# An attention pipeline on one core: order within VectorE's step, units normalized in pairs, lags of 15 and 16 steps, three key or value units a step

## The reference, cut to what matters

```python
x = x + xattn(layernorm(x), ctx, ctx, Wq, Wk, Wv, Wo)   # x: 16 x 512 x 512, ctx: 16 x 120 x 512
x = x + ffn(layernorm(x), w_gate, w_up, w_down)         # inner width 1536, quantized steps
# xattn: 16 heads of 32; q and k are rotated (rope) before the scores
score = einsum('bhqd,bhkd->bhqk', qh, kh) / sqrt(32)
out   = einsum('bhqk,bhkd->bhqd', softmax(score), vh)   # then times Wo
# ffn: rounds x, up, gate, sigmoid(gate), gate*sig and gate*up to 16 bits, each with
# a scale from the largest magnitude of the whole tensor; weights to 4 bits in blocks of 32
```

## Time and profile before

| | us |
|---|---|
| median of three executions | 2526.41 |
| lowest, highest | 2521.74, 2530.59 |
| the profiled execution, its own time | 2532.82 |
| its span in the trace | 2530.9 |
| attention stage in it, up to the gate product's first matmul | 980.5 |

### The profile page before, as it was taken

One profiled execution on the slowest core, in us unless ns is written; L12 is line 12 of the kernel. 1 busy time (PEld: TensorE's weight loads), 2 busy tenths in 40 slices (PEclk: granted clock), 3 DMA queues, 4 the chain that ended last, 5 costly groups with the idle time before them and its releaser, 6 DMA issues.

```text
span 2530.9 us, 32312 instructions
## 1 busy us (share of the span) xinstructions
PE 2271.9 (90%) x12763; PEld 1005.0 (40%) x12763; DVE 1704.4 (67%) x1750; ACT 1285.3 (51%) x1184; POOL 627.8 (25%) x432
## 2 busy tenths in 40 slices
PE   5788887888788876999999989999999499999999
PEld 2443333333333322444444434444444244444444
DVE  5655776677677554664555348988888787777773
ACT  3334443444344311232232248778888597777771
POOL 3542443344334220110010015444444100000000
PEclk9988998999899988999999999999999799999999
DMA  7434445544544455779787569777787465555551
GB/s 206 114 91 119 131 124 145 150 133 128 148 148 125 147 149 161 224 230 290 246 258 245 183 202 369 291 284 283 289 289 290 185 234 216 216 216 218 223 222 69
DMA packets 307913, 505.57 MB, mean 200 GB/s; under 512 B 208172, under 2 KB 210476, under 8 KB 270892
## 3 DMA queue, kind: packets, MB, share of 16 engines
q1 hardware_dynamic: 307756, 503.45, 60.3%
HBM read 248.83 MB, written 186.65 MB: 172 GB/s over the span
## 4 chain that ended last, share of the span: by engine, by line
PE 66%; DVE 13%; DMA 7%; SPq 6%; issue 4%; ACT 2%; POOL 1%; DVEq 0%; POOLq 0%; ACTq 0%
PE banks L1220 39%; PE banks L1617 18%; DMA RB<-sr_s 4%; SPq L344 3%; DVE MX L967 2%; PE banks L562 2%; DVE XA L841 2%; SPq L354 2%; PE banks L520 2%; DVE RX L942 1%; DMA RG<-sr_s 1%; PE banks L483 1%; DVE st L825 1%; PE banks L480 1%; PE banks L539 1%
## 5 line engine op out<-in xcount | busy, mean ns | idle before, releaser
L1617 PE MATMUL banks<-W,OH 128*128 128x512 f16 x2304 | 500.9, 381 | 37.1 <-DVE OH L1696 37.1
L1220 PE MATMUL banks<-XB,W 128*128 128x512 f16 x2304 | 499.3, 380 | 22.7 <-DMA XB<-XC 22.7
L1220 PE MATMUL banks<-XB,WT 128*128 128x512 f16 x2304 | 499.9, 380 | 8.2 <-DMA XB<-xt_s 8.2
L1240 ACT ACTIVATE OB<-banks,uns 128x512 f32<-128x512 f32 x384 | 254.2, 683 | 427.7 <-PE banks L1220 421.1
L1617 PEld LDWEIGHTS banks<-W,OH 128*128 128x128 f16 x2304 | 226.0, 98 | 311.9 <-issue 39.1
L1220 PEld LDWEIGHTS banks<-XB,W 128*128 128x128 f16 x2304 | 225.8, 98 | 296.2 <-DMA XB<-XC 23.2
L1220 PEld LDWEIGHTS banks<-XB,WT 128*128 128x128 f16 x2304 | 225.9, 98 | 282.1 <-DMA XB<-xt_s 8.7
L562 PE MATMUL banks<-XC,AH 128*128 128x512 f16 x768 | 214.6, 439 | 106.5 <-DVE RX L942 106.5
L1485 POOL TENSOR_TENSOR PR<-GS,OB 128x2048 f32<-128x2048 f32 x47 | 226.2, 4814 | 273.0 <-ACT OB L1240 253.6
L1309 DVE TENSOR_REDUCE amx<-OB 128x1 f32<-128x2048 f32 x48 | 109.7, 2285 | 240.5 <-ACT OB L1240 240.5
L520 PE MATMUL banks<-XD,WQ 128*128 128x512 f16 x768 | 178.6, 383 | 0.0
(11 more groups left out here) (211 smaller groups left out, 2944.4 us busy)
## 6 DMA issues: line engine op xcount, KB each, us to landing
g_s<-OB SPq DMA_DIRECT2D x48, 1024.0 KB, 5.7
GL<-g_s SPq DMA_DIRECT2D x48, 1024.0 KB, 8.4
up_s<-OB SPq DMA_DIRECT2D x48, 1024.0 KB, 4.9
XA<-up_s SPq DMA_DIRECT2D x32, 1024.0 KB, 9.3
gq_s<-GQ SPq DMA_DIRECT2D x48, 512.0 KB, 5.1
XD<-gq_s SPq DMA_DIRECT2D x48, 512.0 KB, 6.7
XA<-in_x SPq DMA_DIRECT2D x16, 1024.0 KB, 7.6
QW<-QE SPq DMA_DIRECT2D x128, 128.0 KB, 2.8
```

Source lines behind the costliest of these rows:

```text
L1220: t = e.matmul(pk[:].rearrange("p (j t) -> p j t", j=4), WT[w][:, ot, wa, kk, :], XB[i % 2][:, xa, :, kk, :], start=(kk == 0 and wa == 0 a ...
L1240: e.activation(OB[n % 3][:, r, :], bank[k % 8][:], ACT.Copy, scale=uns[:, 12 * w + ot:12 * w + ot + 1]).then_inc(s_ev, 1)
L1617: t = e.matmul(pk[:].rearrange("p (r n) -> p r n", r=4), OH[i % 2][:, a, ot, j * 128:(j + 1) * 128], WD[:, :, c, wa, o4, :], start=(ot == ...
```

## The change

It rewrites the schedule of the attention stage and leaves the arithmetic as it is.

1. VectorE's step begins with X1, then the rotation's addition, then the normalization, then the statistics of X1. X1 and the output projection belong to units s-16 and s-15 (before: s-18 and s-17). The loop has 80 steps.
2. Units are normalized in pairs: two at c = 1 and two at c = 2 of a step, none at c = 3 and c = 0. Their broadcasts are issued one step earlier at the head of SP's step, eight DMAs together; the store of the reciprocals at c = 3 moves ahead of the transposing DMA and the load of x.
3. Key and value units: 8, then 3 in each of steps 0 to 6, 2 and 1 in steps 7 and 8. The largest magnitudes and splits that belong to them move with them (ctx3 to steps 1 and 2, Wo to 8 and 9, V to 9 and 10).
4. The first four rotations have four buffers (`qe`); the first swaps stand ahead of the first transposing DMA of x; the first loads wait for one another; GpSimd's two rotation products are split, with the low parts between them.
5. The transposing DMAs of the weights and loads of X1 for the next stage move two steps earlier, like `dve_normal` (68, 69 for 72, 74).

```diff
-NSTEP = NU + 18
-KV_STEPS = {-1: 8, 0: 3, 1: 3, 2: 2, 3: 2, 4: 2, 5: 2, 6: 2, 7: 2, 8: 2, 9: 2, 10: 2}
-AMAX = ("ctx0", "wk", "wv", "ctx1", "wq", "ctx2", "ctx3", "v", "wo")
+NSTEP = NU + 16
+KV_STEPS = {-1: 8, 0: 3, 1: 3, 2: 3, 3: 3, 4: 3, 5: 3, 6: 3, 7: 2, 8: 1}
+AMAX = ("ctx0", "wk", "wv", "ctx1", "wq", "ctx2", "ctx3", "wo", "v")
...
+def normal_at(s):
+
+    b, c = divmod(s - 13, 4)
+    return [4 * b + 2 * c, 4 * b + 2 * c + 1] if 0 <= b < B and c < 2 else []
...
+        def qe(n):
+            return (QE[0], QE[1], QR[6], QR[7])[n] if n < 4 else QE[n % 2]
...
         def kv_bank(i):
-            return 5 if i >= 24 or i % 2 == 0 else 6
+            return 5 if i >= 29 or i % 2 == 0 else 6
...
             sp_ctx_load(e, 0)
+            e.wait_ge(s_cx, 16)
             e.dma_start(WLD[0], wk.rearrange("(k p) e -> p k e", p=128)).then_inc(s_wld[0], 16)
             sp_x_load(e, 0)
+            e.wait_ge(s_wld[0], 16)
             e.dma_start(WLD[1], wv.rearrange("(k p) e -> p k e", p=128)).then_inc(s_wld[1], 16)
...
             sp_swap(e, 0, 4 * SK)
+            sp_swap(e, 1, 4 * SK)
             sp_x_turn(e, 0)
             sp_x_load(e, 1)
-            sp_swap(e, 1, 4 * SK)
...
-
-                u = s - 16
+                for u in normal_at(s + 1):
+                    sp_recip(e, u)
+
+                u = s - 14
...
-                u = s - 18
+                u = s - 16
                 if 0 <= u < NU:
                     e.wait_ge(s_x1, u + 1)
                     e.dma_start(x1_d[u // 4, :, u % 4, :], X1[u % 2]).then_inc(s_x1d[u % 2], 16)
...
-                if s == 1:
+                if s == 0:
                     sp_ctx_turn(e, 2)
                     sp_ctx_load(e, 3)
-                if s == 5:
+                if s == 3:
                     sp_ctx_turn(e, 3)
-                if s == 10:
+                if s == 7:
                     e.wait_ge(s_v, 12)
...
+                if c == 3 and 0 <= b - 2 < B:
+                    e.wait_ge(s_rr, 2 * (b - 1))
+                    e.dma_start(sr_d[1 + b % 2].rearrange("r (e f) -> (r e) f", f=64), RG[:]).then_inc(s_rd, 16)
 
                 if c == 1 and 1 <= b + 1 < B:
                     sp_x_turn(e, b + 1)
                 if c == 2 and 2 <= b + 2 < B:
                     sp_x_load(e, b + 2)
-                if 0 <= s - 12 < NU:
-                    sp_recip(e, s - 12)
...
-                if 0 <= s - 17 < NU:
-                    pe_output(e, s - 17)
+                if 0 <= s - 15 < NU:
+                    pe_output(e, s - 15)
...
-                u = s - 13
-                if 0 <= u < NU:
+                for u in normal_at(s):
                     nb, nc_ = divmod(u, 4)
                     e.wait_ge(s_an, u + 1)
...
             for s in range(NSTEP):
                 b, c = divmod(s, 4)
 
-                if s == 0:
-                    dve_x_shift(e, 1)
-                elif s <= NU:
-                    dve_rope_add(e, ROT["q", s - 1])
...
-                u = s - 18
+                u = s - 16
                 if 0 <= u < NU:
                     ob, j = divmod(u, 4)
                     e.wait_ge(s_o, u + 1)
...
                     e.scalar_tensor_tensor(X1[u % 2], BO_, vun[:, 2:3], XR[u % 2], ALU.mult, ALU.add).then_inc(s_x1, 1)
+
+                if s == 0:
+                    dve_x_shift(e, 1)
+                elif s <= NU:
+                    dve_rope_add(e, ROT["q", s - 1])
+                    for i in kv_at(s - 1):
+                        if i % 8 < 4:
+                            dve_rope_add(e, ROT["k", i])
+
+                for u in normal_at(s):
+                    e.wait_ge(s_rb[u % 2], 64 * (u // 2 + 1))
+                    e.wait_ge(s_a, u + 1)
+                    e.tensor_tensor(A[:, u % 6, :], A[:, u % 6, :], RB[u % 2][:], ALU.mult).then_inc(s_an, 1)
...
-                if s in (3, 5, 7):
-                    dve_v_max(e, (s - 3) // 2)
+                if s in (2, 4, 6):
+                    dve_v_max(e, (s - 2) // 2)
...
             for s in range(NSTEP):
                 b, c = divmod(s, 4)
-                u = s - 13
-                if 0 <= u < NU:
+                if s < NU:
+                    pool_rope_cosine(e, ROT["q", s])
+                for u in normal_at(s):
...
                 if s < NU:
-                    pool_rope(e, ROT["q", s])
+                    pool_rope_sine(e, ROT["q", s])
```

More of the change, by code:

```diff
@@ L468, in pe_kv @@
             pk = bank[kv_bank(i)]
-            before = i - 1 if i > 24 else i - 2
+            before = i - 1 if i >= 29 else i - 2
             if before >= 0:
@@ L609, in pe_attention @@
                     pe_queries(e, s)
-                if s == 0:
[L611 to L614, removed]
+                if amax is not None:
+                    if amax == 7:
+                        kv_empty(e, 31)
+                    pe_amax(e, amax)
                 for i in kv[:1]:
@@ L618, in pe_attention @@
                     pe_largest(e, s - 2)
-                if s in (5, 11, 12):
-                    pe_amax_all(e, {5: 6, 11: 7, 12: 8}[s])
+                if amax is not None:
+                    pe_amax_all(e, amax)
                 if c == 2 and 0 <= b - 1 < B:
@@ L645, in act_rope_in @@
         def act_rope_in(e, n):
-            if n >= 2:
-                e.wait_ge(s_rm1, n - 1)
-                e.wait_ge(s_qw[n % 2], 32 * (n // 2))
+            if n >= 4:
+                before = n - 4 if n < 6 else n - 2
+                e.wait_ge(s_rm1, before + 1)
+                e.wait_ge(s_qw[n % 2], 32 * (before // 2 + 1))
         def act_kv(e, i):
@@ L970, in dve_attention @@
                     dve_ctx_low(e, 2)
-                if s == 5:
+                if s == 1:
+                    dve_ctx_max(e, 3)
+                if s == 2:
                     dve_ctx_unit(e, 3)
@@ L1043, in pool_rope @@
                 to = KR[i // 8][:, i % 8, :].rearrange("p (b s) -> p b s", b=4)
-                cc, ss = (a[:].unsqueeze(1).to_broadcast([128, 4, SK]) for a in (ck, sk))
+                cc = ck[:].unsqueeze(1).to_broadcast([128, 4, SK])
             e.wait_ge(s_qe, n + 1)
@@ L1049, in pool_rope, with pool_rope_sine @@
                 e.wait_ge(s_c1, i - 7)
-            e.tensor_tensor(to, v(QE[n % 2]), cc, ALU.mult).then_inc(s_rm1, 1)
+            e.tensor_tensor(to, v(qe(n)), cc, ALU.mult).then_inc(s_rm1, 1)
+        def pool_rope_sine(e, n):
+            what, i = ROTS[n]
+            if what == "q":
+                v, ss = (lambda a: a[:]), sq[:]
+            else:
+                v, ss = (lambda a: a[:, 0:4 * SK].rearrange("p (b s) -> p b s", b=4)), sk[:].unsqueeze(1).to_broadcast([128, 4, SK])
             e.wait_ge(s_qw[n % 2], 32 * (n // 2 + 1))
@@ L1076, in pool_attention @@
             pool_deviation(e, 0)
[L1077 to L1079 removed]
+            pool_rope_cosine(e, 0)
+            pool_rope_sine(e, 0)
+            pool_rope_cosine(e, 1)
+            pool_rope_sine(e, 1)
+            pool_rope_cosine(e, 2)
+            pool_rope_sine(e, 2)
             pool_deviation(e, 1)
[L1081 removed]
+            pool_rope_cosine(e, 3)
+            pool_rope_sine(e, 3)
             for s in range(NSTEP):
                 b, c = divmod(s, 4)
[L1084 to L1085 removed]
+                if s < NU:
+                    pool_rope_cosine(e, ROT["q", s])
+                for u in normal_at(s):
                     nb, nc_ = divmod(u, 4)
@@ L1089, in pool_attention @@
                 if s < NU:
-                    pool_rope(e, ROT["q", s])
+                    pool_rope_sine(e, ROT["q", s])
                 for i in kv_at(s):
                     if i % 8 < 4:
-                        pool_rope(e, ROT["k", i])
+                        pool_rope_cosine(e, ROT["k", i])
+                        pool_rope_sine(e, ROT["k", i])
                 if c == 3 and 2 <= b + 2 < B:
                     pool_deviation(e, b + 2)
-                u = s - 21
-                if c == 1 and 0 <= u < NU:
+                u = s - 19
+                if c == 3 and 0 <= u < NU:
                     ob = u // 4
```

83 lines of the change are left out of this document (34 added, 49 removed).

## The result

The changed kernel takes 2437.73 us (median of four, 2434.03 to 2446.60) against 2528.01 us before: a ratio of 0.9652, 95% interval 0.9619 to 0.9684. That is 90 us less. The forecast was 2396, its range 2355 to 2448; the direction held and the gain was 90 where 130 to 132 were expected, close to the time of the second rival (2433), but for another reason. The profiled execution took 2446.6 us, the longest of the four and 8.9 above their median, with a span of 2444.7.

What follows compares the result with a forecast made beforehand. Attention was taken to lose 11.06 of 50.04 us a sequence above PE's floor, mostly waiting for RB and X1. Steady steps -94, first steps -22 and end -16 sum to -132, giving 2396 us, range 2355 to 2448.

Steps and rivals of the forecast that it cites:

- the second rival: Steady attention steps: the swap comes late twice a sequence, behind broadcasts and transposing DMA; 45 us a sequence, 2433 us; chance 0.20.
- What bounds the kernel, and what goes: Attention stage: 11.06 of 50.04 us a sequence lost, mainly to waits for RB and X1; both ends of X1's wait go.
- What is late next: Steady steps, c = 1: swap behind eight broadcasts lands late, delaying MX; PE waits 1.6 us at the scores of c = 3.
- 38.98 + 1.6 + 1.0 = 41.6: Steady sequence in us: PE's floor, plus its wait for MX, plus lost clock; taken as 41.5, giving -94 over twelve sequences.
- rotation sum, two products 0.7 + 1.4: VectorE's work after the late swap at c = 1, part of 6.2 us up to the end of MX at 638.8.
- No cost: POOL's split and order: GpSimd's split and reordered rotation products in attention cost nothing, since POOL is busy only 183.52 of 450.37 us.
- First steps, -22: Start of attention: 15.5 us from the wait for ctx3, 6 from four first buffers and earlier swaps.
- The bound of +5: Start of attention: worst case of the first-steps term, if the rotations of three units a step bind; best case -35.
- the sign that the prediction named for itself: Start of attention: first steps longer than 177 us would make the prediction wrong.
- The end, -16: End of attention: 54.5 us from last sums to last projection becomes 40.7, two fewer steps give 2; bounds -8 and -22.
- Rival 3: Steady steps: the wait only moves from projection to scores; 50 us a sequence stays, 2488 us; chance 0.06.
- Clock: Steady attention steps: PE's granted clock rises from 0.92 to above 0.95 in the changed profile.

Runs made afterwards that it cites:

- experiments 1: Kernel before, with only X1 moved to the head of VectorE's step: 2482.18 us, ratio 0.9814.
- experiment 2: Kernel before, with X1 first and one unit's broadcasts a step moved to the head of SP's step, no pairs, old lags: 2441.90 us, ratio 0.9653.
- experiment 3: Changed kernel, with the queries' swap put ahead of the eight broadcasts in steps with c = 1: 2427.01 us, ratio 0.9598.
- experiment 6: Changed kernel with old orders before step 0 and the swap ahead of the broadcasts: 2410.60 us; also with the transposing DMA behind the c = 2 swap: 2415.88 us.

## Why the prediction was right or wrong

- **What bounds the kernel, and what goes:** right. The waits for RB and X1 are gone from the trace, and experiments 1 and 2 put 3.6 and 2.9 us a sequence on X1 first and on the early broadcasts (49.44 for the kernel before between the same marks, 45.88, 42.95). The prediction treated the two with the pairs as one step; the pairs turned out to add some tenths of a us to about 1 a sequence there, if anything.
- **What is late next:** right in place and chain (swap behind eight broadcasts, sine product, rotation sum, MX, scores of c = 3), short in size. The term "38.98 + 1.6 + 1.0 = 41.6" measured 42.96 in the long profiled execution and 41.8 to 42.3 in six kernels with the same steady program. The landing was 2.2 to 4.4 us, 2.9 on average, and so well sized at 2.8. The mis-sized term is "rotation sum, two products 0.7 + 1.4": it took 1.63 + 2.35 = 4.0 in every sequence, 1.9 more than written. The low part of x, 3.42 in the rows and 2.35 here, gave back 1.1 of VectorE's time ahead of it; that went into its wait (1.5 to 4.3 us, not 1.7). "No cost: POOL's split and order" is in doubt for the same reason: the sum is long where GpSimd runs beside it (last section).
- **First steps, -22:** wrong, and the largest miss: +7.0. "So I take the 15.5, nothing else here, and 6 from four first buffers and swaps ahead of the transposing DMA" failed in its second half. The wait for ctx3 shrank by 11 us and three units, with the reductions that move along, gave 9 to 10 together, but the orders before step 0, which the sum held to be a gain of 6, cost 12 to 13. Of that the waits between loads, put down as "at most 3 us", cost 3.2 to 3.4. The bound of +5 was too narrow by 2, and the sign that the prediction named for itself, first steps longer than 177 us, came true.
- **The end, -16:** -15.1 up to the gate, the size that was forecast. From the mark of step 66 on it is 19.2 us less than before, of which about half, 9.7, is what lags and pairs give (experiment 2); the early broadcasts and X1 give the rest.
- **The rivals:** the second's time came true, 2433, by luck: its late swap costs PE time at one step of a sequence rather than two (42.96 and not 45), and its other terms had the first steps 29 us too short. The time lies in the range, 10 us from its upper end; of the 44 us by which the stage's gain falls short (88 of 132), 29 are the first steps. The Trainium skill, DMA: Bandwidth & Descriptors, section "Queues, rings and completion order", says that a DMA engine consumes a ring's descriptors in order; by the prediction's reading of it the swap waits for the bytes of the eight broadcasts ahead of it. The traces don't show such a wait: with the swap ahead of them (experiment 3) it still took 2.9 to 4.8 us to land in the seven steps c = 1 in which GpSimd waited for it, no less than the 2.2 to 4.4 behind them. What the change of order saves is the issue time of the broadcasts, 3.6 to 5.0 us. Rival 3 was real in part: with X1 first alone the wait moved to the scores.
- **Clock:** forecast above 0.95 in the steady part, 0.96 measured (0.92 before), 1.00 in experiment 6, where no wait of PE for MX was longer than 1.3 us (4.1 here).

## What to carry to other kernels

Before a wait is priced, write down the order of every in-order queue around it: here two moves, X1 to the head of VectorE's step and the broadcasts ahead of a transposing DMA, gave nearly the whole steady gain, and pairs and lags mainly shortened the end. Price each reordering of a start by itself: one that removes the longest wait can hide others that push back the first transfer on which everything hangs. When a sum is written for an engine that gets a burst of work, ask who else will run beside it. And before two profiled executions are compared, see where each lies among the times of its kernel: here one lay 8.9 us above its median, as much as some of the effects in question.

## What the runs showed of the hardware that was not expected

VectorE's sums and products with both inputs in SBUF stretch when GpSimd's run beside them. The rotation sum takes 656 to 693 ns in the steady part of the kernel before (44 of them) and up to 1630 in the changed one; the pair of products 1.28 us alone and 2.35 when GpSimd's product runs beside it. In the timeline above GpSimd is at L1137 from 455.66 to 456.81, and the sum that starts at 455.73 ends at 457.36, 0.55 us after GpSimd's end. The Trainium skill, SBUF — State Buffer, section "SBUF: two separate sides", says that these two engines take a shared pair of ports in turns, each for a whole instruction, when VectorE's operation has two SBUF inputs and GpSimd's reads SBUF; the trace agrees: 1.63 us is about the rest of GpSimd's operation (1.08) and most of the sum's own 0.68.

The same can be read in the kernel before. The low part of x takes 3.42 us in the earlier trace rows, where GpSimd's sine product starts 0.23 us behind it and takes 2.10 in place of 1.27, and 2.35 where that product starts at 427.69, near its end:

```profile
425.74 2.35 DVE L841 SCALAR_TENSOR_TENSOR XA<-XA 128x1024 f16<-128x1024 f32 x2
```

In experiment 2, which keeps GpSimd's old order and one unit a step, all 44 rotation sums of the steady part take 673 to 694 ns, though VectorE waits for the sine product there as well. With the changed order and pairs the long sum comes in every sequence, and VectorE is busy 387.59 / 11 = 35.2 us of one in place of 376.59 / 11 = 34.2. Which of the two, the pairs or GpSimd's order, brings the engines together was not run by itself.

The first load was hardly faster for being alone: the context's reduction starts at 7.82 us in the changed kernel, where the next load waits for it, and at 8.18 before, where six more loads have been issued behind it by then.

```profile
7.82 2.29 DVE L785 TENSOR_REDUCE amc<-AH 120x1 f32<-120x2048 f32 x1 [3.99 <-DMA AH<-in_ctx]
```
